# Setup, scatter table and the first attention's prologue as one program, with the table's work spread over the prologue and the first score slots

## The reference, cut to what matters

```python
x = x + tanh(g_xattn[0]) * L0_xattn(layernorm(x), ctx, pos, ...)  # 32 heads, rotary positions
x = x + tanh(g_ffn[0])   * L0_ffn(layernorm(x), ...)              # 16 experts, 4 chosen, and a shared one
x = x + tanh(g_xattn[1]) * L1_xattn(layernorm(x), ctx, ...)
x = x + tanh(g_ffn[1])   * L1_ffn(layernorm(x), gate_w, W, atoms, expert_atom_weights, importance, mask_idx)

# L0_xattn, x [8, 256, 512], ctx [8, 256, 256]
q = rope(x @ Wq, pos); k, v = split(ctx @ Wkv); k = rope(k, pos)
out = softmax(q k^T * scale) v @ Wout + bout

# L1_ffn
deltas = softmax(expert_atom_weights) @ atoms            # [8, 4096]
weighted = deltas * sigmoid(importance)                  # [8, 4096]
rows, cols = mask_idx // 512, mask_idx % 512
# expert e's map is W with weighted[e, s] added at (rows[s], cols[s]);
# a token's output is the sum of the maps of its 2 experts, weighted, applied to it
```

## Time and profile before

| | us |
|---|---|
| median of 3 runs (2077.33 to 2079.27) | 2079.18 |
| the profiled execution, its own time | 2078.01 |
| its span in the profile | 2076.2 |
| first two blocks and their barriers, 0 to 55.5 | 55.5 |
| prologue, 55.5 to the first maxima | 38.4 |
| first batch of slots, 93.9 to 163.1 | 69.2 |
| the other seven batches, 163.1 to 627.5 | 464.4 |
| tail of the attention and its barrier, to 646.0 | 18.5 |
| everything after it | 1430.2 |

### The profile page before, as it was taken

One profiled execution on the slowest core, in us unless ns is written; L12 is line 12 of the kernel. 1 busy time (PEld: TensorE's weight loads), 2 busy tenths in 40 slices (PEclk: granted clock), 3 DMA queues, 4 the chain that ended last, 5 costly groups with the idle time before them and its releaser, 6 DMA issues. The chain is left out here.

```text
span 2076.2 us, 38678 instructions
## 1 busy us (share of the span) xinstructions
PE 1843.8 (89%) x11487; PEld 1407.4 (68%) x11487; DVE 1178.7 (57%) x2618; ACT 928.4 (45%) x2627; POOL 962.2 (46%) x1012
## 2 busy tenths in 40 slices
PE   4599999999986999999999999995689999886992
PEld 1355665666554999999999999993356566555881
DVE  5566677767653776433333343334777777764445
ACT  4267676767652332233333333321366666641110
POOL 1487777876741066133433334332455555311660
PEclk9899999999987999999999999998899999996996
DMA  8578877787755426589999988544345454529657
GB/s 324 183 233 271 255 224 249 248 261 229 224 159 171 155 63 206 165 248 269 296 319 280 281 247 248 114 77 112 83 94 117 105 115 101 131 94 374 233 163 273
DMA packets 233756, 414.81 MB, mean 200 GB/s; under 512 B 44289, under 2 KB 121225, under 8 KB 228242
## 3 DMA queue, kind: packets, MB, share of 16 engines
q1 hardware_dynamic: 167194, 324.12, 49.0%
q0 software_dynamic: 30592, 62.54, 13.1%
q10 hardware_dynamic: 35776, 25.69, 4.0%
HBM read 211.97 MB, written 157.82 MB: 178 GB/s over the span
## 5 line engine op out<-in xcount | busy, mean ns | idle before, releaser
L705 ACT ACTIVATE a_P<-a_SC,a_nm 128x256 f32<-128x256 f32 x512 | 235.9, 473 | 130.4 <-DVE a_nm L607 129.6
L1227 POOL DMA_INDIRECT b_y_rows<-b_ysb,b_entry x79 | 124.4, 1575 | 334.6 <-ACT b_ysb L1375 182.2
L607 DVE TENSOR_REDUCE a_nm<-a_SC 128x2 f32<-128x512 f32 x256 | 164.8, 685 | 142.2 <-PE a_SC L838 142.2
L570 POOL TENSOR_TENSOR a_praw<-a_praw,a_phigh 128x704 f32<-128x704 f32 (+2 forms) x126 | 191.8, 1523 | 10.3
L1479 DVE TENSOR_TENSOR b_xl<-b_XT,b_xh 128x512 fp32r<-128x512 f32 x97 | 67.1, 692 | 216.8 <-ACT b_xh L1381 216.3
L849 PEld LDWEIGHTS a_T<-ident,a_P 128*128 128x128 f32 x1024 | 118.5, 144 | 79.6 <-issue 46.3
L849 PE MATMUL a_T<-ident,a_P 128*128 128x128 f32 x1024 | 145.3, 280 | 20.9 <-DVE a_PT L619 17.8
L568 POOL CAST a_phigh<-a_praw 128x704 fp32r<-128x704 f32 (+2 forms) x126 | 111.3, 883 | 100.2 <-DMA a_praw<-in_L_ffn_wd 34.2
L2212 ACT ACTIVATE c_P<-c_SC,c_nm 128x240 f32<-128x240 f32 x256 | 115.7, 457 | 75.8 <-DVE c_P L2084 75.8
L1485 DVE TENSOR_TENSOR b_al<-b_AT,b_ah 128x384 fp32r<-128x384 f32 x111 | 61.9, 558 | 150.0 <-ACT b_ah L1386 150.0
L1375 ACT ACTIVATE b_ysb<-b_Y 128x512 f32<-128x512 f32 x79 | 47.2, 598 | 222.2 <-PE b_Y L1322 212.3
(11 more groups left out here) (494 smaller groups left out, 4923.6 us busy)
## 6 DMA issues: line engine op xcount, KB each, us to landing
w_parts<-a_phigh SPq DMA_DIRECT2D x72, 352.0 KB, 3.7
w_parts<-a_praw SPq DMA_DIRECT2D x72, 352.0 KB, 4.1
b_wh<-w_parts SPq DMA_DIRECT2D x18, 1216.0 KB, 10.3
b_wl<-w_parts SPq DMA_DIRECT2D x18, 1216.0 KB, 13.8
c_q<-c_qT SPq DMA_DIRECT2D x64, 256.0 KB, 4.2
c_k<-c_kT SPq DMA_DIRECT2D x124, 128.0 KB
b_wh<-w_parts SPq DMA_DIRECT2D x18, 704.0 KB, 4.7
b_wl<-w_parts SPq DMA_DIRECT2D x18, 704.0 KB, 7.3
```

Source lines behind the costliest of these rows:

```text
L570: eng.tensor_tensor(raw[:, 0:k * m], raw[:, 0:k * m], r32(high[:, 0:k * m]), ALU.subtract).then_inc(plow_done, 1)
L607: eng.tensor_reduce(nm[:, g % 4, j, :], SC[j][:, :].rearrange("p (t k) -> p t k", t=BT), AX.X, ALU.max, negate=True).then_inc(topped, 1)
L705: e = eng.activation(Pr[:, i, t, :], SC[j][:, t * S:(t + 1) * S], ACT.Exp, bias=nm[:, g % 4, j, t:t + 1], accum_out=den[:, h, t:t + 1])
L1227: eng.indirect_dma_start(out=y_rows, out_offset=bass.IndirectOffsetOnAxis(ap=entry[:, r, 1:2].bitcast(U32), axis=0), in_=ysb[:, v % RING, ...
```

## The change

The three blocks become one. `setup` and `scatter_tables` go; `rope_attention` does their work inside its slots. The first batch gets order tables of its own (`FIRST_ITEMS_AT` and so on), the splitting of weights starts at slot 10 instead of -6 and is spread up to slot 129, x is loaded in pieces and its statistics are taken in five portions. W is turned into the banks of the scores and the turned exponentials before the first score, so TensorE waits at s = -2 for all eight half-maps (`wide_ready`). The half-maps are sent by ScalarE's own queue. The rotary angles move from VectorE to GpSimd. The work on single places is divided in new items: `E` (the weights), `match` and `earlier` (the comparisons, 8 portions of 128 x 512 each), `S0` and `S1` (the sums).

```diff
-    angles_ready = 2 * HALF // 2 + 1 + 6
+    angles_ready = HALF + 1 + 8
...
-def rope_attention(nc, core, ctx_d, pos, Wq, Wkv, Wout, bout, gate, add_column, columns_added, split):
+def rope_attention(nc, core, x, ctx_d, pos, Wq, Wkv, Wout, bout, g_xattn, g_ffn, placing, table, split):
...
+    FIRST_ITEMS_AT = {-15: ("X0", "X1"), -14: ("Q0",), -13: ("K0",), -12: ("Q1",), -11: ("q0a",), -10: ("K1",),
+                      -9: ("V0", "k0a"), -8: ("q1a",), -7: ("V1",), -6: ("q0b", "k0b"), -5: ("q1b",), -4: ("E",),
+                      -3: ("k1a",), -2: ("k1b",), 4: ("S0",), 6: ("S1",),
+                      **{s_: ITEMS_AT[s_] for s_ in (28, 29, 30, 31, 32)}}
...
-    SPLIT_AT, NRAW, NHIGH = -6, 4, 3
+    FIRST_ROTATE_AT = {-14: 0, -13: 1, -12: 2, -10: 3}
...
+    SPLIT_AT, SPLIT_END, NRAW, NHIGH = 10, END + 1, 4, 3
+    SECOND_TOKENS = -1
...
+    EARLY_AT = {-15: (1,), -14: (2,), -13: (3,), -12: (4,), -10: (5,), -8: (6,), -6: (7,)}
+    MATCH_AT, MATCHES = 1, 2
...
+    def split_before(s):
+
+        return min(max(0, (s - SPLIT_AT) * split.count // (SPLIT_END - SPLIT_AT)), split.count)
...
         @block.sync
+            eng.dma_start(ea[:, 0, :], eaw).then_inc(ea_in, 16)
+            eng.dma_start(core.X[:, 0:BT, :], xf[:, 0:BT, :]).then_inc(x_in[0], 16)
             load_positions(eng)
+            eng.dma_start(Wraw[:, :, :], maps_W.rearrange("(r p) c -> p r c", p=P)).then_inc(W_in, 16)
             eng.dma_start(wq[:, :, :], kview(Wq)).then_inc(wq_in, 16)
             context(0)
             eng.dma_start(wkv[:, :, :], kview(Wkv)).then_inc(wkv_in, 16)
+            eng.dma_start(core.X[:, BT:2 * BT, :], xf[:, BT:2 * BT, :]).then_inc(x_in[1], 16)
...
+            def late_loads(s):
+                if s == -7:
+                    for i in range(3):
+                        q = slice(4 * i + 4, 4 * i + 8)
+                        eng.dma_start(core.X[:, q, :], xf[:, q, :]).then_inc(x_in[i + 2], 16)
+                if s == -4:
+                    for i in (3, 4):
+                        eng.wait_ge(wide_out[i], WIDE_OUT[i])
+                    eng.dma_start(row_i[:, :, :].rearrange("p c q -> p (c q)"), mask_idx.partition_broadcast(P)).then_inc(rows_in, 16)
...
         @block.gpsimd
+            angles(eng)
+            eng.memset(V[0][:, :, :], 0.0).then_inc(consts, 1)
...
         @block.vector
+            eng.wait_ge(x_in[0], 16)
+            layer_norm_scales(eng, vseq, c, core.X, core.st, llw, lnsc, slice(0, BT))
...
+            eng.wait_ge(idx_in, 16)
+            eng.tensor_copy(idx_f[:, :], idx_r[:, :]).then_inc(pseq, 1)
...
+            def later_stats(s):
+                if s in range(0, NT // 2 - 2):
+                    t = 2 * s + 4
+                    eng.wait_ge(x_in[t // 4 + 1], 16)
+                    for t in (t, t + 1):
+                        eng.bn_stats(core.st[:, t, :], core.X[:, t, :]).then_inc(vseq, c.inc())
+                if s == NT // 2:
+                    eng.wait_ge(vseq, c.now)
+                    layer_norm_scalars(eng, vseq, c, core.st, llw, lnsc, slice(2 * BT, NT))
...
             for s in range(FIRST, LAST):
+                if s == -11:
+                    addresses()
+                if s == -3:
+                    place_weights()
+                if s == 5:
+                    place_half(0)
+                if s == 7:
+                    place_half(1)
+                if s == -6:
+                    second_stats()
...
+                later_stats(s)
+                for j in range(MATCHES * (s - MATCH_AT), MATCHES * (s - MATCH_AT + 1)):
+                    if 0 <= j < C // MATCH:
+                        match(j)
...
         @block.scalar
+            def widen(h):
+                k, part, i = h // 2, slice(RH * (h % 2), RH * (h % 2 + 1)), KEPT_IN[h]
+                eng.wait_ge(maps_turned, k + 1)
+                if KEPT_IN.index(i) < h:
+                    eng.wait_ge(wide_out[i], 16)
+                eng.activation(wide[i][:, :, :], map_bank[k][:, part].unsqueeze(2).to_broadcast([P, RH, E]),
+                               ACT.Copy).then_inc(wide_ready, 1)
...
         @block.tensor
+            for k in range(KD):
+                turn_maps(k)
             for s in range(FIRST, LAST):
...
+                if s == -2:
+                    eng.wait_ge(wide_ready, 8)
```

More of the change, by code:

```diff
@@ L282, in angles @@
[L282 to L289, removed]
@@ new lines, in angles @@
+        eng.wait_ge(adone, a.now)
+        eng.tensor_scalar(U, U, MAGIC, None, ALU.add).then_inc(adone, a.inc())
+        eng.wait_ge(adone, a.now)
+        eng.tensor_scalar(U, U, -MAGIC, None, ALU.add).then_inc(adone, a.inc())
+        for part in (HI, LO):
+            eng.wait_ge(adone, a.now)
+            eng.tensor_scalar(V, U, -part, None, ALU.mult).then_inc(adone, a.inc())
+            eng.wait_ge(adone, a.now)
+            eng.tensor_tensor(A, A, V, ALU.add).then_inc(adone, a.inc())
+        eng.wait_ge(adone, a.now)
@@ L365, in items, with due @@
         return [(b, n) for b, n, i, j in pieces(s) if j == TERMS.get(n[0], 1)]
-    def due(s, table):
-        return [(b, table[s - PAIRS * b]) for b in range(B) if s - PAIRS * b in table]
+    def split_before(s):
+        return min(max(0, (s - SPLIT_AT) * split.count // (SPLIT_END - SPLIT_AT)), split.count)
+    def due(s, first, others):
+        return [(b, at[s - PAIRS * b]) for b, at in ((b, others if b else first) for b in range(B)) if s - PAIRS * b in at]
     number = {}
@@ L533, in _ @@
         def _(eng):
+            eng.memset(core.ident[:, :], 0.0).then_inc(ident_set, 1)
+            eng.wait_ge(ident_set, 1)
+            eng.affine_select(out=core.ident[:, :], in_=core.ident[:, :], compare_op=ALU.not_equal, fill=1.0,
+                              base=0, pattern=[[-1, P]], channel_multiplier=1).then_inc(ident_set, 1)
             eng.memset(one[:, :], 1.0).then_inc(consts, 1)
-            for i in range(2):
-                eng.memset(V[i][:, :, :], 0.0).then_inc(consts, 1)
+            eng.memset(zeros[:, :], 0.0).then_inc(st_consts, 1)
+            eng.memset(ones_b[:, :], 1.0).then_inc(st_consts, 1)
+            eng.iota(dump_i[:, :], pattern=[[1, C]], base=D * D, channel_multiplier=C).then_inc(st_consts, 1)
+            angles(eng)
+            eng.memset(V[0][:, :, :], 0.0).then_inc(consts, 1)
             def tokens(b):
@@ new lines, in place_weights @@
+            def place_weights():
+                w = bank((0, "E"))
+                filled(eng, (0, "E"))
+                eng.tensor_copy(wgt[:, :, :], w[:, C * E:2 * C * E].rearrange("p (e c) -> p c e", e=E)).then_inc(pseq, cp.inc())
+                eng.wait_ge(pseq, cp.now)
+                eng.tensor_tensor(wgt[:, :, :], wgt[:, :, :], w[:, 0:C * E].rearrange("p (c e) -> p c e", e=E),
+                                  ALU.mult).then_inc(*freed((0, "E")))
+                is_freed(eng, (0, "E"))
+                cur = wgt[:, :, :]
+                left = rest[:, :].rearrange("p (c e) -> p c e", e=E)
+                for i in range(NP):
+                    if i:
+                        eng.wait_ge(pseq, cp.now)
+                    if i == NP - 1:
+                        eng.tensor_copy(parts[:, :, i, :], cur).then_inc(parts_ready, 1)
+                        break
+                    eng.tensor_copy(parts[:, :, i, :], cur).then_inc(pseq, cp.inc())
+                    eng.wait_ge(pseq, cp.now)
+                    eng.tensor_tensor(left, cur, parts[:, :, i, :], ALU.subtract).then_inc(pseq, cp.inc())
+                    cur = left
@@ L680, in _ @@
                         unit(b, n)
-                for b, n in due(s, ROTATE_AT):
+                for b, n in due(s, FIRST_ROTATE_AT, ROTATE_AT):
                     rotate(b, n)
```

498 lines of the change are left out of this document (251 added, 247 removed).

## The result

| | before | after | predicted |
|---|---|---|---|
| median, us (5 runs each) | 2077.42 | 2092.74 | 2051, range 2035 to 2065 |
| lowest and highest | 2076.86, 2079.27 | 2090.33, 2099.09 | |
| first maxima (first L607 or L804) | 93.9 | 60.8 | 53.8 |
| first batch of slots | 69.2 | 88.4 | 80 |
| the other seven batches | 464.4 | 490.7 | 465 |

What follows compares the result with a forecast made beforehand. TensorE was taken to bound the later slots, and a chain of waits the lead-in to the first maxima. Sum: 2078.0 - 40 (lead-in) + 11 (first batch) + 1 (splitting) = 2050, median 2051; range 2035 to 2065 us.

Steps and rivals of the forecast that it cites:

- The splitting of weights: Slots of the attention: 126 pieces over 119 slots, 0.14 us more GpSimd work each, hidden by its room; 1 us counted.
- 17 us as the end: Upper end for the weight splitting over all slots, if GpSimd had no room to hide the extra work.
- The closing sentence of the prediction: Signs of a wrong prediction: maxima waiting on half-maps, clock 0.50 throughout slots 1 to 8, later slots waiting for `a_recw`.
- The first batch: First batch of slots: 10 us more from VectorE's added work and 1 for the index rows; ends 2 and 18.
- the one slot with the norm: Slot 8 of the first batch, carrying the other tiles' norm: 2.1 + 1.5 + 3.7 = 7.3 us of VectorE.
- the rule that I weighed for the first norm: Prologue: VectorE and GpSimd share locked ports, so angles on GpSimd could delay the first norm to 14 us, total 2052.
- First maxima: End of the lead-in: first maxima at 53.8 us instead of 93.9, 40 us earlier.
- The first Q: Early prologue: first product of Q at 16 us, between 14 and 19, GpSimd's angles of 4 to 7 us hidden.
- the half-maps on ScalarE and `addresses` on VectorE: Between first Q and first maxima: 4 us for ScalarE's widening (ends 0 and 11) and 3 for VectorE's `addresses`.
- the tail's sum: From the last low part to first maxima: 10.7 us of VectorE plus a score of 1.2, 11.9 instead of 8.9.
- transfers not binding the lead-in: Rival, chance 0.13: some 17 MB of transfers bound the new lead-in, first maxima at 62 us, total 2059.
- the clock: Rival, chance 0.05: TensorE's idle gaps in the first slots keep its clock low, 7.9 us a slot, total 2098.

Runs made afterwards that it cites:

- e2: The changed kernel with five raw buffers for the weight splitting instead of four, slots with two pieces left in place; 2073.89 us, ratio 0.9975.
- e6: The changed kernel with the second norm's 20 small VectorE steps at slot 6 instead of slot 8; 2090.27 us, ratio 1.0055.
- e10: The changed kernel with five raw buffers, second norm at slot 6, angles on VectorE, late token loads issued first, tiles 4 to 15's statistics in slot -4; 2063.23 us.
- e7: The changed kernel with the rotary angles back on VectorE and the casts that wait for indices behind the first rotation; 2098.19 us, ratio 1.0082.

## Why the prediction was wrong, step by step

**The splitting of weights: +1 predicted, +26 measured.** This is the step that failed, and it decides the sign. I compared GpSimd's busy time with the length of the stretch and called the room a cover; I gave 17 us as the end if there were none. The work was indeed covered (e2 has the same 363 us on GpSimd and 467 in all). What was not covered was a time: a load that must land before one slot, from a ring that was just deep enough for one piece a slot. I worked the average of 126 on 119 slots and did not list which slots get two, nor walk the ring across one. The closing sentence of the prediction named the sign to look for, TensorE waiting for `a_recw`, but gave it no chance and no price. With this step repaired (e2) the time is 2073.89, still above the range, in the main because the next two terms were short as well, by 15 us together.

**The first batch: +11 predicted, +19 measured.** Of the 8 us that were missing, 7.2 are the one slot with the norm, put at 7.3 us and 14.49 long. Without its collision (e6) the batch took 80.8, against 80 predicted. The sum over the other eight slots was right, 44.1 us worked out and 45.6 measured, but single slots were off by up to 1.8 us either way, so that is in part luck. VectorE did bind several of them, as I had it, but not all (e10). The collision is the rule that I weighed for the first norm, and not for this one. The Trainium skill, page "SBUF — State Buffer", section "SBUF: two separate sides", has GpSimd's instructions and some of VectorE's (those with two inputs in SBUF, or in a mode that uses two ports) take turns at a shared pair of ports, the later one blocked for the whole of the other's instruction. Here the trace agrees: steps of 0.17 us became 0.8 to 1.6 beside GpSimd's casts, sums and indirect transfers of 1.3 to 1.8 us, and 0.17 again with it idle. The low parts agree too: up to 1.75 us beside GpSimd's sum and 0.69 without, both before and after. (Of the two that I quoted, the one of 1.03 us stood beside a cast, not an addition.) At the first norm, for which I had weighed it, the trace shows no such hold: the 20 steps took 3.7 us, 0.32 at the longest, though GpSimd worked on the angles beside them.

**First maxima: 40 us earlier predicted, 33 measured.** The missing 7 are the sum of three misses, one of them lucky. The first Q came 4.1 us late, at 20.1 instead of 16: GpSimd's angles took 9.8 us, not 4 to 7, and xn stands behind them and a memset. On VectorE (e7) five of the six one-operand steps of 128 x 256 took 0.29 us; on GpSimd four took 0.85, and one 1.87, beside VectorE's scaling of `a_wq`:

```profile
8.29 0.85 POOL L254 TENSOR_SCALAR rt_turns<-rt_ang 128x256 f32<-128x256 f32 x1
...
12.84 1.87 POOL L261 TENSOR_SCALAR rt_sin<-rt_turns 128x256 f32<-128x256 f32 x1
```

e7 gave 4.05 us back. From the first Q to the end of the last low part it was 19.5 us instead of 18.9 + 4 + 3 = 25.9: the half-maps on ScalarE and `addresses` on VectorE, put at 7 us, cost 0.6. That hid most of the third miss: from there to the maxima it was 21.2 us instead of 11.9, 9.3 more. That is E, whose matmuls the tail's sum left out. I let VectorE run from the last low part to the maxima, with TensorE free beside it. It wasn't:

```profile
44.22 4.38 PE L1080 MATMUL a_W<-a_eaT,st_atoms 64*128 64x8 f32 x32
...
48.93 6.99 PE L1080 MATMUL a_W<-a_eaT,st_atoms 64*128 64x8 f32 x32
...
55.96 0.42 DVE L738 COPY st_wgt<-a_W 128x256 f32<-128x256 f32 x1 [10.31 <-PE a_W L1080]
```

The windows of the same stretch show why the second half cost 6.99 us instead of 4.38:

```profile
44.00:48.00 4.00, 4.00 (x33) 3.87 (x32) 1.40 (x6) 3.57 (x4) 1.52 (x2) 0.89 1.01 311
48.00:52.00 4.00, 4.00 (x19) 3.75 (x19) 0.00 (x0) 0.07 (x1) 0.00 (x0) 0.50 0.94 310
```

**What held:** the first batch without the norm, as a sum, the exchange hidden in the prologue, the index wait (3.4 us) hidden behind the first Q, transfers not binding the lead-in (share 0.85 at 295 GB/s, but no map was waited for at its end). Of the rivals the clock came nearest, for another reason than mine and in other slots.

## What to carry to other kernels

When work is spread by an integer division over slots, list the slots that get one more and walk the buffers across such a slot: busy time against span does not see it. Before moving work under an engine's idle time, ask what stands behind it in that queue and which engine waits for that; in the slot from pair 66 to 67 a wait of 3.3 us on TensorE cost nearly as much again at the lower clock. And test a large change's by-products alone: here two numbers changed in the kernel before (the start of the splitting and a fifth buffer) gave as much, 2064.1 us, as the whole merged program with its faults repaired, 2064.2.

## What the runs showed of the hardware that was not expected

- On GpSimd the number of operands did not tell the price. Steps with one operand and one operation took 0.85 us for 128 x 256 float32, 2.9 times VectorE's 0.29 (e7). Steps with one operand and two operations were far cheaper: the clamp of the same size took 0.40, and the tokens (`a_xn`) 0.77 for 128 x 512, the row from which I had priced the angles. Its two-operand sum of 128 x 256 took 0.72, 1.7 times VectorE's 0.42. Why one operation costs more than two is not shown.
- A matmul with 64 x 128 stationary and 8 moving columns in float32 took 4.38 us for 16 products (32 in the row) while the granted clock was between 1.00 and 0.89, 0.27 us each, though it moves next to nothing; PEld, the loading of the stationary side, was busy for 3.87 of 4 us there. The granted clock fell to 0.50 in the middle of them, while the profile has TensorE busy for 4.00 of every 4 us; the same 16 products then took 6.99 us, 0.44 each.
- Twenty VectorE steps of 0.17 us took 11.0 us beside GpSimd's casts, sums and indirect transfers, three times their 3.5, but 3.7 us beside its steps on the angles.
- In one slot TensorE's idle 3.3 us were followed by four at a granted clock of 0.50, and the slot was 6 us longer than before.
